# Two column blocks of 256 in place of the first block of 512, with the early rounds placed between the next blocks' units

## The reference

```python
# layer 0, u and i are the first 2048 and the other 3072 rows of x
e = concatenate([par_u[0] * par_u[1] * (diag_u[:, None] * x_u @ W_u) + x_u,
                 par_i[0] * par_i[1] * (diag_i[:, None] * x_i @ W_i) + x_i])
h = adj @ (adj.T @ e)
out = layernorm(h) * gamma + beta + x
x1 = layernorm(x + out)
# layer 1: a message pass over the edges of adj that survive pruning
return layernorm(x1 + message(x1, adj))
```

## Time and profile before

| | us |
|---|---|
| median of three runs | 396.67 |
| lowest and highest | 395.41, 396.76 |
| the profiled execution | 397.39 |
| its span, first to last instruction | 395.5 |

### The profile page before, as it was taken

One profiled execution on the slowest core, in us unless ns is written; L12 is line 12 of the kernel. 1 busy time (PEld: TensorE's weight loads), 2 busy tenths in 40 slices (PEclk: granted clock), 3 DMA queues, 4 the chain that ended last, 5 costly groups with the idle time before them and its releaser, 6 DMA issues.

```text
span 395.5 us, 13309 instructions
## 1 busy us (share of the span) xinstructions
PE 379.0 (96%) x5762; PEld 220.2 (56%) x5762; DVE 316.7 (80%) x305; ACT 269.1 (68%) x519; POOL 63.8 (16%) x122
## 2 busy tenths in 40 slices
PE   8987999999999999999999999999999999999990
PEld 7743655565465546545654664565466456555770
DVE  1699989797697869687976989697698869795674
ACT  3598996994868658597856868685876778511143
POOL 2001101102100300030030003003000300277375
PEclk9999999999999999999999999999999999999996
DMA  8999999995797799579877958996795799400012
GB/s 291 387 388 382 386 386 384 386 352 192 232 380 267 268 320 391 180 275 389 314 263 272 386 195 277 388 351 230 278 386 191 272 392 383 145 3 2 24 35 85
DMA packets 56991, 109.83 MB, mean 278 GB/s; under 512 B 3808, under 2 KB 4576, under 8 KB 56928
## 3 DMA queue, kind: packets, MB, share of 16 engines
q1 hardware_dynamic: 56640, 108.84, 76.3%
q10 hardware_dynamic: 288, 0.09, 0.1%
HBM read 107.60 MB, written 1.31 MB: 275 GB/s over the span
## 4 chain that ended last, share of the span: by engine, by line
PE 84%; DMA 6%; issue 3%; DVE 3%; POOL 1%; ACT 1%; SPq 1%; POOLq 0%; DVEq 0%
PE quad L1491 45%; PE quad L1471 34%; DMA pooled<-in_adj 6%; PE quad L1506 2%; DVE pooled L1265 2%; PE quad L1513 1%; PE quad L1442 1%; ACT scratch L1153 1%; SPq L1033 1%; PE quad L1452 1%; DVE pooled L1285 1%; POOL pooled L1112 1%; POOL col_sum L1084 0%; POOLq L96 0%; POOL pooled L1107 0%
## 5 line engine op out<-in xcount | busy, mean ns | idle before, releaser
L1153 ACT ACTIVATE scratch<-pooled 128x1024 bf16<-128x1024 f32 x200 | 210.1, 1051 | 39.8 <-DMA pooled<-in_adj 38.0
L1265 DVE STREAM_TRANSPOSE pooled<-pooled 128x1024 f32<-128x1024 f32 x200 | 229.7, 1209 | 3.3 <-ACT scratch L1153 3.2
L1471 PE MATMUL quad<-pooled,rows_in 128*64 128x256 f32 x1600 | 180.2, 381 | 4.3 <-DMA pooled<-in_adj 4.3
L1491 PE MATMUL quad<-pooled,col_sum 32*64 32x320 f32 (+4 forms) x3968 | 177.5, 507 | 0.4 <-POOL col_sum L1084 0.2
L1471 PEld LDWEIGHTS quad<-pooled,rows_in 128*64 128x64 f32 x1600 | 111.9, 137 | 74.3 <-issue 13.1
L1491 PEld LDWEIGHTS quad<-pooled,col_sum 32*64 32x64 f32 x3968 | 87.5, 132 | 83.1 <-issue 64.6
L1285 DVE TENSOR_TENSOR pooled<-pooled,quad 128x1280 f32<-128x1280 f32 (+5 forms) x29 | 52.4, 1808 | 43.8 <-PE quad L1491 43.7
L1084 POOL COPY col_sum<-col_half 32x256 f32<-32x256 f32 x80 | 31.6, 394 | 312.1 <-DVE col_half L1274 309.0
L1162 ACT COPY col_sum<-col_half 32x256 f32<-32x256 f32 x80 | 32.2, 402 | 38.0 <-DVE col_half L1274 37.0
L1153 ACT ACTIVATION_READ_ACCUMULATOR scratch<-pooled 128x1 f32 x200 | 37.4, 187 | 0.0
L1183 ACT ACTIVATE pooled<-quad 128x256 f32<-128x256 f32 (+2 forms) x7 | 3.3, 475 | 23.4 <-PE quad L1506 23.4
(11 more groups left out here) (45 smaller groups left out, 62.8 us busy)
## 6 DMA issues: line engine op xcount, KB each, us to landing
pooled<-in_adj SPq DMA_DIRECT2D x200, 512.0 KB, 9.4
pooled<-in_x SPq DMA_DIRECT2D x5, 256.0 KB, 3.7
pooled<-in_x SPq DMA_DIRECT2D x1, 768.0 KB, 5.3
pooled<-in_x SPq DMA_DIRECT2D x1, 512.0 KB, 3.8
out<-pooled SPq DMA_DIRECT2D x2, 256.0 KB, 2.5
out<-pooled SPq DMA_DIRECT2D x2, 192.0 KB, 2.4
out<-pooled SPq DMA_DIRECT2D x3, 128.0 KB, 2.1
pooled<-in_w_ui ACTq DMA_DIRECT2D x1, 64.0 KB, 3.3
```

Source lines behind the costliest of these rows:

```text
L1153: nc.scalar.activation(scratch[v % 2][:, :], slots[slot_of(v)], ACT.Square, accum_out=square_sum[:, v:v + 1]).then_inc(unit_scanned, 1)
L1265: nc.vector.transpose(tiles, tiles).then_inc(unit_turned, 1)
L1471: mm = pe.matmul(block_bank(c)[half(h), 0:w // 2], rows_in[:, t, :], slots[slot_of(v)][:, at:at + w // 2], start=(t == 0), stop=(t == T - 1))
L1491: mm = pe.matmul(round_banks(g)[a][half(b % 2), 0:w].rearrange("p (t r) -> p t r", r=32), col_sum[c % 2][quadrant(a), b, :], to[quadrant(a ...
```

## The change

The first 512 columns become two blocks of 256, so there are 11 blocks; the number of units stays 200. A unit of a block of 256 has four row tiles, and such a block has 10 units and rounds of 8, 16 and 16 tiles, of 64 instructions each. The two small blocks use slots 20 to 29 and 30 to 39. The orders of VectorE and TensorE are written out for blocks 0 to 3: the rounds of a block stand among the units of the next one, each followed by units, and the loop starts two blocks later in number (one block of 512 later in columns). Rounds 0 to 5 use the upper banks, 6 to 8 the lower. Block 2's product is in bank 0 like block 1's.

```diff
@@ -31,7 +31,7 @@
     THETA = [0.000244 + (1.0 - math.exp(-0.1 * it)) * (0.0003 - 0.000244) for it in range(ROUNDS)]
 
 
-    WIDTHS = (512,) * 10
+    WIDTHS = (256, 256) + (512,) * 9
     NB = len(WIDTHS)
     COL_FIRST = [sum(WIDTHS[:c]) for c in range(NB)]
     SLOT = 1024
@@ -41,10 +41,10 @@
     UNITS = UNIT_FIRST[NB]
 
     SLOTS = 40
-    SLOT_FIRST = [20 if c % 2 == 0 else 0 for c in range(NB)]
+    SLOT_FIRST = [20, 30] + [0 if c % 2 == 0 else 20 for c in range(2, NB)]
     assert sum(WIDTHS) == N and max(WIDTHS) == CH
 
-    PARTS = [((0, 10), (10, 14), (24, 16))] * (NB - 1)
+    PARTS = [((0, 8), (8, 16), (24, 16))] * 2 + [((0, 10), (10, 14), (24, 16))] * (NB - 3)
     PARTS += [((0, 12), (12, 12), (24, 8), (32, 8))]
 
 
@@ -368,10 +368,15 @@
 
 
 
             c = place_of_round(g)[0]
             if c == NB - 1:
                 return banks_of_block(c) == (g == LAST)
-            return banks_of_block(c + 1) == (0 < c < NB - 2 and g == ROUNDS_AT[c + 1] - 1)
+            return banks_of_block(c + 1) == (2 < c < NB - 2 and g == ROUNDS_AT[c + 1] - 1)
+        def product_in_banks_before(c):
+            return max((b + 1 for b in range(c) if banks_of_block(b) == banks_of_block(c)), default=0)
 
         def products_in_banks(g):
 
@@ -1020,11 +1025,11 @@
             for v in range(UNITS):
                 c, i = place_of_unit(v)
                 ut, c0 = UNIT_TILES[c], COL_FIRST[c]
-                if v == UNIT_FIRST[1]:
+                if v == UNIT_FIRST[2]:
                     sp.dma_start(gamma_sb[:, :], gamma).then_inc(norm_in, 16)
                     sp.dma_start(beta_sb[:, :], beta.partition_broadcast(P)).then_inc(norm_in, 16)
 
-                    assert SLOT_FIRST[1] == 0 and SETUP_SLOTS <= UPB[1]
+                    assert SLOT_FIRST[2] == 0 and SETUP_SLOTS <= UPB[2]
                     sp.wait_ge(e_made, LGROUPS)
                 before = before_in_slot(v)
                 if before:
@@ -1171,7 +1176,7 @@
                 scan(v)
                 if i == UPB[c] - 1:
                     keep_cols(c)
-                if c == 1 and i == 16:
+                if c == 2 and i == 16:
                     act.wait_ge(gamma_turned, 1)
                     act.copy(center[:, D:2 * D], bank[3][:, 0:D]).then_inc(center_kept, 1)
 
@@ -1290,34 +1295,60 @@
             make_e(0)
             make_e(1)
             make_e(2)
-            for v in range(3):
-                turn_unit(v)
+            turn_unit(0)
             make_e(3)
-            for v in range(3, 7):
-                turn_unit(v)
+            turn_unit(1)
             make_e(4)
-            for v in range(7, UPB[0] - 4):
+            for v in range(2, 6):
                 turn_unit(v)
             turn_half(0)
-            for v in range(UPB[0] - 4, UPB[0]):
+            for v in range(6, UNIT_FIRST[1]):
                 turn_unit(v)
 
 
-            turn_unit(UNIT_FIRST[1])
+            first = UNIT_FIRST[1]
             add_round(0)
-            make_gamma_and_beta()
-            for v in range(UNIT_FIRST[1] + 1, UNIT_FIRST[1] + 9):
+            for v in range(first, first + 4):
                 turn_unit(v)
             add_round(1)
-            for v in range(UNIT_FIRST[1] + 9, UNIT_FIRST[1] + 16):
+            for v in range(first + 4, first + 8):
                 turn_unit(v)
             turn_half(1)
-            for v in range(UNIT_FIRST[1] + 16, UNIT_FIRST[2]):
+            for v in range(first + 8, first + 10):
                 turn_unit(v)
             add_round(2)
-
-
-            for c in range(1, NB - 1):
+            first = UNIT_FIRST[2]
+            make_gamma_and_beta()
+            for v in range(first, first + 4):
+                turn_unit(v)
+            add_round(3)
+            for v in range(first + 4, first + 10):
+                turn_unit(v)
+            add_round(4)
+            for v in range(first + 10, first + 15):
+                turn_unit(v)
+            add_round(5)
+            turn_unit(first + 15)
+            turn_half(2)
+            for v in range(first + 16, first + 20):
+                turn_unit(v)
+            first = UNIT_FIRST[3]
+            for v in range(first, first + 8):
+                turn_unit(v)
+            add_round(6)
+            for v in range(first + 8, first + 14):
+                turn_unit(v)
+            add_round(7)
+            for v in range(first + 14, first + 17):
+                turn_unit(v)
+            add_round(8)
+            turn_unit(first + 17)
+            turn_half(3)
+            for v in range(first + 18, first + 20):
+                turn_unit(v)
+            for c in range(3, NB - 1):
                 first = UNIT_FIRST[c + 1]
                 for v in range(first, first + 13):
                     turn_unit(v)
@@ -1460,7 +1491,7 @@
                 wait_loaded(pe, v)
                 if i == 0 and c >= 2:
 
-                    pe.wait_ge(halves_turned_b, c)
+                    pe.wait_ge(halves_turned_b, product_in_banks_before(c))
                     same = before_in_banks(ROUNDS_AT[c - 1], banks_of_block(c))
                     if same:
                         pe.wait_ge(round_added, same[-1] + 1)
@@ -1529,21 +1560,45 @@
                     multiply_unit(v)
 
 
-            for v in range(UNIT_FIRST[1], UNIT_FIRST[1] + 2):
-                multiply_unit(v)
+            first = UNIT_FIRST[1]
+            multiply_unit(first)
             multiply_round(0)
-            for v in range(UNIT_FIRST[1] + 2, UNIT_FIRST[1] + 9):
+            for v in range(first + 1, first + 4):
                 multiply_unit(v)
             multiply_round(1)
+            for v in range(first + 4, first + 10):
+                multiply_unit(v)
+            multiply_round(2)
+            first = UNIT_FIRST[2]
+            for v in range(first, first + 7):
+                multiply_unit(v)
+            multiply_round(3)
             pe.wait_ge(gamma_made, 1)
             pe.matmul(bank[3][:, 0:D], center_t[:, :], center_g[:, :], start=True, stop=True).then_inc(gamma_turned, 1)
-            for v in range(UNIT_FIRST[1] + 9, UNIT_FIRST[2]):
+            for v in range(first + 7, first + 12):
                 multiply_unit(v)
-            multiply_round(2)
-
-
-
-            for c in range(1, NB - 1):
+            multiply_round(4)
+            for v in range(first + 12, first + 17):
+                multiply_unit(v)
+            multiply_round(5)
+            for v in range(first + 17, first + 20):
+                multiply_unit(v)
+            first = UNIT_FIRST[3]
+            for v in range(first, first + 8):
+                multiply_unit(v)
+            multiply_round(6)
+            for v in range(first + 8, first + 14):
+                multiply_unit(v)
+            multiply_round(7)
+            for v in range(first + 14, first + 17):
+                multiply_unit(v)
+            multiply_round(8)
+            for v in range(first + 17, first + 20):
+                multiply_unit(v)
+            for c in range(3, NB - 1):
                 first = UNIT_FIRST[c + 1]
                 for v in range(first, first + 16):
                     multiply_unit(v)
```

## The result

The changed kernel takes 395.07 us, the median of 20 runs, against 396.16 us of the kernel before beside it. The ratio is 0.9969 with a 95% interval of 0.9959 to 0.9980: 1.2 us faster (0.8 to 1.6), a third of the 3.8 us that were forecast. Two more rounds of comparisons gave 0.9977 (0.9967 to 0.9987) and 0.9965 (0.9946 to 0.9985). One of the 20 runs took 1019.7 us, the only such run in this study, for a reason not known; the ratio leaves it out, and the other 19 lie between 393.97 and 397.05.

What follows compares the result with a forecast made beforehand. TensorE, busy for 96% of the span, was taken as the bound. The median 396.67 less 3.1 us from the earlier first round and 0.7 us of late load waits gave 392.9 us, range 391.3 to 396.3.

Steps and rivals of the forecast that it cites:

- where TensorE was idle: TensorE: 5.6 us idle before the first round, and 1.4 us of late load waits in blocks 3 and 4.
- VectorE's list: VectorE's ordered work in the ramp: half transposes near 24.5 and 42 us, no stall, last four additions 0.2 or 0.3 us spare.
- rival 2: VectorE paces the ramp: additions 5 to 8 come late and TensorE waits; one or two us easily lost, chance 12%.
- the copies of 0.33 us: Column copies on ScalarE and GpSimd: eight more, of 128 elements, taken at 0.33 us each instead of 0.41.
- Rival 4: Later blocks: TensorE comes 3 us earlier, waits in more of them for loads, gain given back; 396.5 us, chance 5%.
- I take nothing: Loads of the first 20 units: 1 KB rows instead of 2 KB priced at no extra time; bounds nothing and twice the time.
- rival 3: First 20 loads: 1 KB rows load slowly; loss 27.1 s - 3 us for a slowdown share s, chance 7%.
- margin of 3 us: Unit 47's load, the tightest: lands at 74 us and is wanted at 76.9.
- The walk: Step-by-step schedule of TensorE, VectorE and loads: round 0 at 26.4 us, unit 60 at 105.9 instead of 108.98, 3.1 us gained.
- Four copies end at 26.2, round 0 starts at 26.4: Start of the first round: half transpose done at 24.75 us, then four copies; TensorE idle 1.2 us in place of 5.6.
- A narrow unit was taken at 0.97 us: TensorE's 256-wide units: 16 instructions at 61 ns, 0.07 to 0.10 us more than now, about 1.4 us for 20.
- The late waits: Load waits in later stretches, 1.4 us in the profiled execution, should go in units 60 to 79; 0.7 counted against the median.

Runs made afterwards that it cites:

- the loop experiment: Changed kernel with the loop starting one block earlier, block 2's rounds after 16 and 20 units of block 3: ratio 1.0049 to the kernel before.
- the better order: Changed kernel with units 10 and 11 ahead of round 0 in TensorE's list: ratio 0.9961 to the kernel before; with 2 KB rows 0.9933.
- the execution run again: Profiled execution of the changed kernel measured once more, nothing changed: ratio 0.9977 to the kernel before.
- the kernel with the narrow block: Kernel before with block 5's product in narrow matmuls, 128 columns at a time instead of 256, 304 instructions for 152: ratio 1.0023.

## Why the prediction was wrong

**What was right.** The bound; where TensorE was idle; that the first round comes near 27 instead of 39.9, and the order of all rounds after it; VectorE's list, for which TensorE waits 0.2 us at most in the changed kernel's profile (rival 2 did not come); the copies of 0.33 us. Rival 4, waits for loads in later blocks, did not come either: from 105 to 365 us TensorE is held up by a load in one of the changed kernel's four profiles, by 0.4 us. Spreading block 2's rounds keeps the loads out of TensorE's way; the loop experiment puts that at 3.1 us.

**The step that failed first: "I take nothing" for the 1 KB rows.** The term was taken from a load of 64 KB that shared the engines with others, which says how soon a small load lands and nothing of a rate. It measured 0.15 us a load, 11%, 3 us over the 20. With the old rows in the changed kernel about 1.2 us come back (give or take 0.9), so this term is about half of the 2.6 us between the gain that was forecast, 3.8, and the 1.2 that came. It is rival 3 in its mild form. The estimate from the Trainium skill (DMA: Bandwidth & Descriptors, Why small descriptors are slow) had 4 or 5%: the right sign, and under half the size. The bounds in the text, nothing and twice the time, held the value, but the sum used the lower end. Rival 3 was priced with a loss that begins only when a margin of 3 us is used up; at 11% that rule says zero loss (27.1 x 0.11 - 3), which is how the cost stayed out of the sum.

**The margin itself was the second error.** The walk checked the loads against TensorE at loads of 1.35 us only. At 1.50 us unit 9 starts at 23.0 to 23.5, when its load lands and not when TensorE is free; and the lag of 3 us, with a gap of 1 us on top, uses up the whole margin of unit 47. The row for this is unit 39 at 67.0 in place of 63. In the changed kernel that cost 0.2 us in two executions of four, but it bars the way to more: a kernel whose TensorE comes to unit 47 sooner waits there for its load. With 2 KB rows and the better order, which multiplies the wrong data, the walk's 105.9 was reached (105.7), and the ratio, 0.9933, is 2.7 us.

**The end of round 0.** "Four copies end at 26.2, round 0 starts at 26.4", and ends 1.86 us later: the second half of the round needs the other four copies, which end at 27.26 in the changed kernel (24.64 + 2.62). In the execution run again the round starts at 26.31, waits 0.22 us inside and ends at 28.71: 2.40 us in place of 1.86, and 0.4 later than in the walk.

**Terms of the sum that had the wrong size.** A narrow unit was taken at 0.97 us; six of them take 5.39, so 0.90, the lower bound, and the kernel's 320 narrow instructions show in its groups by form:

```profile
L1502 PE MATMUL quad<-pooled,rows_in 128*64 128x128 f32 x320 | 19.5, 275 | 3.0 <-DMA pooled<-in_adj 3.0
```

(275 ns is the modelled length of one; two stream side by side, and they come every 56 to 58 ns.) That is 0.5 us back from round 0 on. Against it, every turn from units to a round and back costs about 0.1 us that the walk left out: by the rows a group of n units takes 0.87 n + 0.1, a round of 64 instructions on 512 columns 3.62 us (31.74 to 35.36), not 3.53. From round 0 to unit 60 this makes about 1.1 us (78.2 - 77.6 + 0.5). Added up for the execution run again: round 0 ends 0.4 us later than in the walk, the stretch from there to unit 60 takes 78.2 us instead of 77.6, and 106.9 is 1.0 later than 105.9.

**The late waits.** The forecast counted 0.7 us of them against the median. With the loads halved they weigh 0.2 (at most 0.6). Such waits come and go between executions (the profile of the kernel with the narrow block has one of 0.27 us at 229.52), and the execution that the forecast was made against had 1.4 us of them. What could have told it was the table of runs: the profiled time was 0.7 us above the median of three, and is 1.2 above that of 20.

The account, in us: 3.8 forecast; 0.5 less for the late waits; 1.4 less in the ramp, 1.7 by the means of the profiles in place of 3.1. That leaves 1.9, and 1.2 (0.8 to 1.6) were measured. The last 0.7 are not accounted for; single executions of either kernel differ by 1 to 2 us, in pauses of TensorE and load gaps of no fixed place, and in the landing of the last store.

## What to carry to other kernels

When a block is made narrower so that work can start sooner, price the shorter rows of its loads by a run with the new row length in the old kernel, since the ramp is the one place where loads are the bound, and carry the lag through to every later point at which the consumer takes units in a row. A short round meets its producer twice, at its start and at its half, and taking the unit of ready work in front of it away cost 1.3 us here, with the clock at half for 3.4 us. And a wait found in one profiled execution need not be in the median: halve the loads, or whatever feeds it, and see.

## What the runs showed of the hardware

- Loads of 512 KB from HBM in rows of 2 KB ran at 382 to 387 GB/s, in rows of 1 KB at 347 to 350, in both kernels and with either order of work. From 1.355 us for 256 rows and 1.50 us for 512 on 16 engines, a fixed part of 9 ns for each row and 38 ns for each KB is an estimate; only two lengths were measured.
- A float32 matmul instruction with 64 weight columns on 128 streamed columns comes every 56 ns, half of the one on 256. The loads of weights, 137 ns each, stay hidden, although both halves have the same rows of the array. The Trainium skill (TensorE: Matmul & The Clock Gate, The mechanism) has loads overlap only with matmuls on other rows; for these column halves the trace speaks against it.
- TensorE's granted clock fell from 2.4 to 1.2 GHz at about 27.6 us in the profile in which it was busy for 0.27 us from 24 to 26 and for 1.59 from 26 to 28, and came back at 31.0. With 0.12 and then 1.97 us (the changed kernel), and with 0.62 and then 1.61 us (2 KB rows), it stayed at 2.4.
- In most executions one of the first loads came 0.4 to 1.5 us behind the pace of the rest: unit 10, 16 or 20, by kernel. Why was not found.
